# A decoder kernel's output: 64 indirect scatters from GpSimd in place of 16 plain stores from SyncE

## The reference

```python
h = jax.nn.gelu(jnp.einsum('bsd,edh->bseh', x, up_w))            # 8 experts, hidden width 512
expert_outputs = jnp.einsum('bseh,ehd->bsed', h, down_w)
output = jnp.sum(topk_weights[:, :, :, None] * gathered, axis=2)   # 4 of 8 experts per token
...
x = x + _L1_ffn_ref(_layernorm(x, axis=-1), ...)
return x
```

## Time and profile before

| | us |
|---|---|
| median of 3 runs | 2620.15 |
| lowest and highest of them | 2616.71, 2621.27 |
| span of the profiled execution (its own time; no other is recorded for it) | 2623.9 |
| granted TensorE clock, mean over the span | 0.950 |
| TensorE busy | 2352.1 (90%) |
| VectorE busy | 2079.6 (79%) |
| ScalarE busy | 1965.4 (75%) |
| GpSimd busy | 835.8 (32%) |

### The profile page before, as it was taken

How to read it: one execution, slowest core, us unless ns; L and a number is a source line. 1 busy time by engine, 2 the same in 40 slices (tenths; PEclk the granted TensorE clock), 3 DMA queues, 4 the chain that set the end, 5 groups by cost and what they waited for, 6 DMA issues and landing times.

```text
span 2623.9 us, 95406 instructions
## 1 busy us (share of the span) xinstructions
PE 2352.1 (90%) x34892; PEld 1856.2 (71%) x34892; DVE 2079.6 (79%) x5391; ACT 1965.4 (75%) x3652; POOL 835.8 (32%) x1203
## 2 busy tenths in 40 slices
PE   2999943967899999999899999899899999999999
PEld 1666632645888888888767666566688788888887
DVE  6788889668899999999667777688766777777776
ACT  1888852777899999999467776788577777777776
POOL 1455510336566666666343333233100000000000
PEclk9999975987999999999899999799799999999999
DMA  5000000000000000000010000111111111111111
GB/s 183 1 0 0 0 16 0 1 0 3 1 0 0 0 0 0 0 0 0 5 63 0 0 0 1 37 42 42 29 45 45 49 57 52 56 50 55 52 56 44
DMA packets 56808, 64.82 MB, mean 25 GB/s; under 512 B 7696, under 2 KB 35088, under 8 KB 56592
## 3 DMA queue, kind: packets, MB, share of 16 engines
q1 hardware_dynamic: 56720, 63.65, 8.1%
HBM read 59.17 MB, written 4.46 MB: 24 GB/s over the span
## 4 chain that ended last, share of the span: by engine, by line
PE 70%; DVE 16%; issue 8%; ACT 2%; SPq 1%; DVEq 1%; POOL 1%; ACTq 0%; POOLq 0%; DMA 0%
PE ps L1064 5%; PE ps L1107 5%; PE ps L1092 5%; PE ps L1337 4%; PE ps L1359 4%; PE ps L1361 4%; PE ps L1360 4%; PE ps L1339 4%; PE ps L1338 4%; PE ps L1237 3%; PE ps L1120 3%; PE ps L1079 3%; DVE work L1813 2%; DVE work L1804 2%; DVE work L1814 2%
## 5 line engine op out<-in xcount | busy, mean ns | idle before, releaser
L557 POOL TENSOR_TENSOR work<-work,consts_sb 128x1024 f32<-128x1024 f32 x128 | 246.0, 1922 | 386.6 <-ACT work L725 346.8
L1249 PE MATMUL ps<-work 32*32 32x32 f32 x16384 | 250.0, 224 | 42.1 <-DVE work L1768 30.1
L1249 PEld LDWEIGHTS ps<-work 32*32 32x32 f32 x16384 | 242.8, 145 | 56.5 <-issue 56.5
L1972 DVE TENSOR_TENSOR h_low<-consts_sb,h_up 128x1024 fp32r<-128x1024 f32 x128 | 156.8, 1225 | 115.7 <-ACT h_up L953 115.7
L1575 DVE TENSOR_REDUCE work<-ps 128x8 f32<-128x512 f32 x256 | 169.9, 686 | 85.8 <-PE ps L1064 80.0
L1337 PE MATMUL ps<-a_low,w_up 128*128 128x512 f32 x512 | 205.9, 402 | 0.0
L1359 PE MATMUL ps<-h_low,d_up 128*128 128x512 f32 x512 | 199.9, 390 | 2.2 <-DVE h_low L1972 2.2
L1339 PE MATMUL ps<-a_up,w_low 128*128 128x512 f32 x512 | 200.7, 392 | 0.0
L1338 PE MATMUL ps<-a_up,w_up 128*128 128x512 f32 x512 | 200.6, 392 | 0.0
L1361 PE MATMUL ps<-h_up,d_low 128*128 128x512 f32 x512 | 199.5, 390 | 0.0
L1972 DVE TENSOR_TENSOR h_low<-small_w,h_up 128x1024 fp32r<-128x1024 f32 x128 | 156.9, 1225 | 53.8 <-ACT h_up L953 53.8
(11 more groups left out here) (296 smaller groups left out, 6353.6 us busy)
## 6 DMA issues: line engine op xcount, KB each, us to landing
gates_spread<-gate_rows SPq DMA_DIRECT2D x128, 256.0 KB, 3.1
ctxT_all<-in_ctxT SPq DMA_DIRECT2D x1, 4096.0 KB, 12.8
work<-in_ctx SPq DMA_DIRECT2D x64, 64.0 KB, 1.8
work<-in_ctxT SPq DMA_DIRECT2D x64, 64.0 KB, 1.8
out<-x_all SPq DMA_DIRECT2D x16, 256.0 KB, 3.6
big<-in_up SPq DMA_DIRECT2D x1, 2048.0 KB, 8.3
consts_sb<-in_consts SPq DMA_DIRECT2D x1, 936.0 KB
w<-in_key_inT SPq DMA_DIRECT2D x1, 512.0 KB, 3.7
```

Source lines behind the costliest of these rows:

```text
L557: pool.tensor_tensor(KX[:, u].rearrange("p b (h k) -> p b h k", h=PER_SET), KC[:, u].unsqueeze(2).to_broadcast([P, 2, PER_SET, SEQ]), own_ ...
L1249: ins = pe.matmul(psW[rows, n // 16, :, n % 16], XT[rows, T.u, :, n], YT[rows, T.u, :, n], start=True, stop=True)
L1972: dve.tensor_tensor(h_low[:, n], hid[n], h_up[:, n].bitcast(F32), ALU.subtract).then_inc(h_split, 1)
```

## The change

A tile `token` of 128 x 64 unsigned integers is added; GpSimd fills it in its first instruction with `p + 128 t`, the number of the output row that belongs to partition `p` of tile `t`. SyncE's `store` segment is taken out of its list, and its last wait counts 64 transfers in place of 16. GpSimd gets, behind its last instruction of before, a stretch written out in full: for each quad a wait for `out_ready`, then four indirect DMAs, each of which scatters the 128 rows of one token tile to the output rows named in one column of `token`.

```diff
+        token = sb("token_rows", [P, NT], U32)
...
+        tokens_ready = sem("tokens_ready")
...
-            def store(T):
-                sp.wait_ge(out_ready, T.now())
-                sp.dma_start(ov.rearrange("p (s t) d -> p s t d", t=QUAD)[:, T.t], xs_quad[:, T.t]).then_inc(stored, 16)
-            staggered(nc, sp, NT // QUAD, [(0, keep_gate_rows), (0, spread_gates), (2, store)])
-            sp.wait_ge(stored, 16 * (NT // QUAD))
+            staggered(nc, sp, NT // QUAD, [(0, keep_gate_rows), (0, spread_gates)])
+            sp.wait_ge(stored, 16 * NT)
...
         def _(pool):
+            pool.iota(token[:, :], [[P, NT]], base=0, channel_multiplier=1).then_inc(tokens_ready, 1)
             pool.memset(less_half[:, :], -0.5)
...
+            pool.wait_ge(tokens_ready, 1)
+            for s in range(NT // QUAD):
+                pool.wait_ge(out_ready, s + 1)
+                for t in range(QUAD * s, QUAD * s + QUAD):
+                    pool.indirect_dma_start(out, bass.IndirectOffsetOnAxis(ap=token[:, t:t + 1], axis=0), xs[:, t, :], None)\
+                        .then_inc(stored, 16)
```

More of the change, by code:

```diff
@@ L498, in _ @@
             staggered(nc, sp, NT, [(0, ctx_load), (0, keys_load)])
-            ov = out.rearrange("(t p) d -> p t d", p=P)
             def keep_gate_rows(T):
```

## The result

The changed kernel takes 2629.69 us (median of 5 runs, 2627.39 to 2635.20) against 2620.15 us before (5 runs, 2616.71 to 2621.27). The ratio is 1.0034, with a 95% interval of 1.0024 to 1.0045: slower by 8.9 us, between 6.3 and 11.8; the medians themselves lie 9.5 us apart. The execution that was profiled took 2627.39 us, the fastest of the five, with a span of 2625.5 us.

The account below looks back on a forecast made before the run. TensorE was taken to bound the kernel, with only the serial tail exposed: 0.05 + 4 x 1.2 + 2.2 + 0.4 = 7.45 us in place of 3.0, so 2620.15 + 4.45 = 2624.6 us; range 2620.5 to 2632.0.

Parts of the forecast that it names:

- no change within 0.2%: Whole kernel: a difference under about 0.2%, 5.2 us, which a measurement cannot tell from no change; chance 0.53, slower 0.42.
- the upper end: Tail, dearest likely case: 1.92 us per scatter, 3.8 us landing, 1 us drain; +9.95 us, 2630.1 us.
- The stage: Mixture stage beside TensorE's work: sixty scatters fit into the 44.0 us of each quad; cost 0.
- SyncE's relief: Sixteen stores leave SyncE's queue, 6.5 us together: worth 0 in the stage; in the tail one 0.4 us issue goes.
- the iota: GpSimd's first instruction, filling the row numbers, 128 x 64 elements: cost 0, covered by the wait for the loads.
- VectorE held up by scatters: Rival in the stage: scatters shut out VectorE, TensorE loses 1.2 us in each of 15 quads, 2642.6 us; chance 0.08.
- c: Time of one scatter on GpSimd, four in a row in the tail: taken at 1.2 us, between 0.4 and 1.92.
- my estimate: Tail reckoned with the skill page's 1 us per scatter: 6.65 us, time 2623.8 us.
- Start, landing, end: Tail: 0.05 us to see the semaphore, 2.2 us for the last scatter to land, 0.4 us to the span's end.
- The drain: GpSimd's drain at the block's end, behind the last scatter: 0, running during the landing; up to 1 us at most.
- Serial scatters: Rival: each scatter waits until the one before has landed, 3.4 us each; +12.4, 2632.6 us; chance 0.07.

## Why the prediction was right or wrong

The forecast was 2624.6 us, +4.5, in a range of 2620.5 to 2632.0; measured were 2629.69. The time lies in the range and the direction of the sum was right. But I gave no change within 0.2% the larger chance (0.53 against 0.42), and it came out slower by more than that. That the time fell into the range is in part luck: the upper end was built from a dearer scatter (1.92 us), a slower landing (3.8 us) and 1 us of drain, and neither of the first two came; the drain alone filled it.

*The stage.* Right. SyncE's relief is worth nothing, the iota costs nothing (0.18 us where a wait for the loads follows), and 60 scatters beside TensorE cost nothing: 644.9 us in both profiles, and the kernel with 60 scatters and a plain last store is no slower than before.

*VectorE held up by scatters.* This rival fell. It needed 0.80 us of delay for each pass; the medians didn't move, and 8 scatters in a row per quad (124 in all) left TensorE's waits at 1.2 us. The worst that a scatter did to a pass of `lower_half` in the changed kernel was 0.075 us, once. The rule that I weighed beside it, from the Trainium skill ("SBUF — State Buffer", section Who interferes with whom), is that a VectorE instruction with two inputs there contends with a GpSimd instruction that reads there, and the first to start shuts the other out. The trace agrees with one half of it for scatters: one that starts inside such a pass ends 0.82 or 0.83 us behind it, at 1.41 or 1.16 us in place of 0.96. It doesn't agree with the other half, a VectorE pass shut out for a scatter's whole length: those that start inside a scatter keep their time.

*c.* Taken at 1.2 us; measured 1.26 us from one scatter to the next (0.96 of work, 0.30 between). The about 1 us of the Trainium skill ("DMA: Bandwidth & Descriptors", section Specifications) is a latency to the first byte; my estimate took it for the time that a scatter keeps GpSimd. That time is near it here, 0.96 us, but 0.30 us more pass before the next.

*Start, landing, end.* Taken at 0.05, 2.2 and 0.4 us; measured 0.28 us to the first scatter, 1.3 us from the last scatter's end to SyncE's release, and, in the kernel before and in the two with an early drain, 0.4 us from there to the end. 0.28 + 4.74 + 1.3 + 0.4 = 6.7 us, against my 7.45. The two kernels with an early drain, which have just these terms, measured 6.7.

*The drain.* This is the step that failed. I wrote "I take 0 for it, because it runs while SyncE waits for the landing, and up to 1 us in the upper end". It does run beside the landing, but it is 5.3 us long with 64 scatters to go through and ends 4 us after it. The row for it was before me, a drain of 1.98 us in the earlier trace rows, but that one only ran beside GpSimd's last short passes and had no DMA behind it; that a drain's length could depend on how many DMAs GpSimd had issued was not in the bounds. The term was mis-sized by 3.8 us (tail 10.5 against 6.7), and the experiments with one drain, with 84 and with 108 scatters show it from both sides. Without it the tail would have grown by 3.7 us, within 0.2%, which is where I had put the larger chance.

*Serial scatters.* They fell too: a scatter starts 0.30 us behind the one before, and 1.0 us before that one's rows land.

What stays open: both measurements of the changed kernel lie 1.5 to 2 us above what its tail explains, which their intervals cover.

## What to carry to other kernels

A transfer that is late costs nothing until the tail, so price the last piece of an output by itself: count how many issues stand one behind the other there, and ask what each engine still has to clear before the block can end. If GpSimd issues DMAs, let it drain once in its idle time before the last of them, or give the last piece to SyncE: either took back the drain here, and the second all of the loss. And when two profiles differ by less than their executions do, compare stages and tails by their own lengths, not the spans.

## What the runs showed of the hardware that I had not expected

- GpSimd's drain ends the later behind its last scatter, the more scatters it has issued since the drain before, even where these landed hundreds of us ago: 5.0 us for 60, 5.3 for 64, 8.9 for 108, about 0.2 us + 0.080 us for each. It doesn't go by rows: 16 plain stores with the same 8192 rows took 2.6 us. Its floor is about 1.5 us, measured with 4.
- With 124 scatters there is, in the one profile, a pause of 3.1 us before the 114th, and afterwards a short drain (1.7 us).
- The first scatter of a kernel starts 0.95 to 0.97 us behind the addition that releases it in place of 0.28. It lasts 1.23 us in place of 0.96 in five profiles, and about 2.28 us in four, where it waits for a pass of VectorE, the second profile of the changed kernel among them.
- A scatter that starts inside a VectorE pass with two on-chip inputs lasts until 0.83 us behind that pass (1.41 us with 0.59 to go, 1.16 with 0.33). Beside a pass with one input in `ps` it keeps its 0.96 us.
- A plain store of 256 KB costs GpSimd 0.75 us, a scatter of 64 KB 0.96 us, and SyncE's store of 256 KB 0.41 us.
